# A graph network's edge products: split bf16 matmuls replaced by float32 matmuls over 64 rows

## The chip, the cores and the metric

One core of one Trainium2 chip. The metric is the device time of one execution in microseconds; the median of three runs of the kernel before is 1686.68 (1679.48 to 1689.82).

## The reference

Three layers of a graph network on 3125 nodes of 128 features, with 53125 directed edges sorted by destination, each with 64 attributes. Everything is float32. For layer k:

```
e   = edge_vector @ edge_W[k] + edge_b[k]      # 53125x64 @ 64x128
msg = relu(x[src] + e)
agg = segment_sum(msg, dst)
z   = (1 + eps[k]) * x + agg
h   = relu(batch_norm(z @ W1[k] + b1[k]))
x   = relu(layer_norm(h @ W2[k] + b2[k]))
```

The end result is the layer norm of the input plus the last x. The change touches how `edge_vector @ edge_W[k]` is computed for all three layers.

## The kernel before

The edges are cut into tiles of 128, four tiles a quad, four quads a block. Blocks alternate between two kinds. Those of kind s have their source rows fetched by one-hot matmuls and for that are re-sorted by source; those of kind p have them gathered by GpSimd's indirect DMAs. Two blocks, one of each kind, are a body; there are 13 bodies, 52 quads of each kind. In what follows "quad n" (0 to 51) means one quad of kind s with one of kind p.

The program has two stages. In the **first** the edge products for all three layers are made at once (64 attributes by 3 x 128 columns), one tile a PSUM bank with 384 columns, four banks for s and four for p:

- SP and ScalarE load the attributes, 64 partitions of 512 edges per kind and quad, three slots for each kind (`load_attr`, line 409).
- TensorE multiplies in bf16. A float32 number is written as a sum of three bf16 parts: the high half of the word is the first part in place, the remainder after it gives the second, the remainder after that the third. VectorE makes the remainders (`split_attr`, lines 958 to 969, two instructions per kind and quad, subtracting and writing the third part into the low halves), ScalarE copies the second and third parts to partitions 64 to 127 (`second_part`, lines 708 to 716, two per kind and quad), so that a matmul contracts 128 rows of two parts at once. The weights are split once (lines 975 to 982). TensorE then takes five accumulating bf16 matmuls per tile (`terms_of`, lines 1549 to 1557).
- Kind s is copied out of PSUM by ScalarE (line 734, all four banks at once), two columns of metadata are appended (line 738), and GpSimd scatters the rows by four indirect DMAs, one per tile, to a table in DRAM in source order (`srt`, line 668). Four buffers in `stage_s`; a quad's buffer is free again when the scatters of four quads earlier have landed.
- Kind p is evicted by VectorE with the bias added (`staged`, line 1124) and stored by SP to `ep` (line 445), with two buffers.
- VectorE has much else to do in between, in an order written out by hand by the quad's number: ranks and positions of the edges for the scatter (lines 1021 to 1055; the first positions before quad 0, lines 1355 to 1358), one-hot matrices (`hots_of`, line 1142; `build_hots`, line 1205), and the three-part split of x (lines 1169 to 1181).
- Before it there is a start: VectorE counts edges by source slice, TensorE ranks them (line 1539), VectorE works out a flag that picks this path or a general one (line 1086), on which all engines wait.
- In bodies 9 to 12 GpSimd's queue also has the four gathers of body 0 (line 652), each between two groups of scatters.

In the **second** stage each layer goes over the 13 bodies: one-hot gathers on TensorE (line 1582), additions on VectorE (lines 1220, 1227), relu on ScalarE (line 748), one-hot scatters on TensorE (line 1599 in bf16 for s, line 1609 in float32 for p), and the small node matmuls (lines 1618, 1625, 1633). Layer 0's later bodies need metadata that is read back after all of the first stage's scatters have landed (`load_meta`, line 454). Every engine runs its own instructions in program order, and semaphores join them.

## Time and profile before

| | |
|---|---|
| median of three runs | 1686.68 us |
| the profiled execution: span, first to last instruction | 1314.0 us |
| its own time beside the span | not given; median less span is 372.7 us |
| TensorE busy | 1201.3 us, 91% |
| VectorE busy | 1049.1 us, 80% |
| GpSimd busy | 886.4 us, 67% |
| ScalarE busy | 686.1 us, 52% |
| mean granted TensorE clock | 0.961 |
| DMA | 310.09 MB, mean 236 GB/s |
| chain that ended last, by engine | PE 46%, POOL 24%, issue 15%, DVE 11%, DMA 4% |

PE is TensorE, DVE VectorE, ACT ScalarE, POOL GpSimd. Busy shares are averages over stages that have different limits, so the rows below are read by stage. The first stage's products run on TensorE from 28 to 385 us; the rest is the three layers. A line in the trace has its start, its duration, the engine and the source line, and in brackets the idle time of that engine before it and what ended it.

### The profile page before, as it was taken

What the parts mean: (1) busy time and instruction counts of PE and PEld (TensorE: products, weight loads), DVE (VectorE), ACT (ScalarE), POOL (GpSimd) and SP (SyncE); (2) the same over time, 40 slices, a digit from 0 to 9 for tenths busy, and PEclk for the clock granted to TensorE, in tenths of its full rate; (3) what the DMA queues carried; (4) which work ended last, traced back from release to release, by engine and by line L of the source; (5) the groups of instructions that cost most, each with busy time, mean ns of one, the idle gap of its engine ahead of it and who ended that gap; (6) DMA issues with size and microseconds to landing.
All of it is one profiled execution on the core that took longest, in us unless ns stands there. A gap on an engine that the chain in (4) does not pass through costs nothing.

```text
span 1314.0 us, 36511 instructions
## 1 busy us (share of the span) xinstructions
PE 1201.3 (91%) x13740; PEld 1016.8 (77%) x13740; DVE 1049.1 (80%) x2020; ACT 686.1 (52%) x1303; POOL 886.4 (67%) x842
## 2 busy tenths in 40 slices
PE   3999999999996899999996899999996899999995
PEld 1555555555566899999986889999985898999994
DVE  8889988899877899998977566767666658788887
ACT  2665666666644466656552344444442434545543
POOL 0555666678777777777725777777762777777770
PEclk8999999999997899999997899999997999999997
DMA  8687888888988888888884777777766677788771
GB/s 181 236 275 259 282 293 284 294 292 266 320 268 266 263 246 251 247 250 245 242 265 139 209 217 228 228 224 228 231 199 181 176 226 211 238 242 250 240 215 35
DMA packets 253577, 310.09 MB, mean 236 GB/s; under 512 B 53837, under 2 KB 170623, under 8 KB 253415
## 3 DMA queue, kind: packets, MB, share of 16 engines
q1 hardware_dynamic: 205646, 212.37, 52.3%
q0 software_dynamic: 33280, 82.06, 19.9%
q10 hardware_dynamic: 14489, 13.40, 4.1%
q8 instruction: 115, 1.88, 0.6%
q14 instruction: 47, 0.39, 0.1%
HBM read 200.17 MB, written 107.55 MB: 234 GB/s over the span
## 4 chain that ended last, share of the span: by engine, by line
PE 46%; POOL 24%; issue 15%; DVE 11%; DMA 4%; ACT 1%; DVEq 0%; ACTq 0%; SPq 0%
POOL rows L652 20%; PE ps L1582 17%; PE ps L1609 6%; PE ps L1599 5%; POOL srt_dram L668 4%; PE ps L1553 3%; PE ps L1555 3%; PE ps L1554 3%; PE ps L1556 3%; PE ps L1557 3%; DMA rows<-table_dram,src_i 3%; DVE terms L966 1%; PE ps L1633 1%; DVE terms L1124 1%; DVE hot_stage L1142 1%
## 5 line engine op out<-in xcount | busy, mean ns | idle before, releaser
L652 POOL DMA_INDIRECT rows<-table_dram,src_i x416 | 431.9, 1038 | 182.0 <-issue 176.8
L668 POOL DMA_INDIRECT srt_dram<-region,pos_i x208 | 230.2, 1107 | 149.2 <-ACT region L738 62.9
L652 POOL DMA_INDIRECT rows<-x_dram,src_i x208 | 222.1, 1068 | 63.4 <-issue 63.4
L1582 PE MATMUL ps<-xs,early_words 125*128 125x128 bf16 x2720 | 253.4, 222 | 10.9 <-issue 10.9
L1582 PE MATMUL ps<-xs,region 125*128 125x128 bf16 x2584 | 242.5, 223 | 11.0 <-issue 10.8
L1582 PE MATMUL ps<-xr,early_words 125*128 125x128 bf16 x1360 | 243.6, 221 | 0.0
L1582 PE MATMUL ps<-xr,region 125*128 125x128 bf16 x1292 | 232.9, 222 | 0.0
L1582 PEld LDWEIGHTS ps<-xs,early_words 125*128 125x128 fp8e4 x2720 | 219.5, 99 | 11.3 <-issue 11.1
L1582 PEld LDWEIGHTS ps<-xs,region 125*128 125x128 fp8e4 x2584 | 209.6, 99 | 11.4 <-issue 11.1
L748 ACT ACTIVATE terms<-terms 128x512 f32<-128x512 f32 x156 | 97.4, 625 | 217.5 <-DVE terms L1220 217.4
L1609 PE MATMUL ps<-hot_p,terms 128*128 128x64 f32 x1248 | 170.5, 281 | 12.9 <-issue 12.3
L1609 PEld LDWEIGHTS ps<-hot_p,terms 128*128 128x128 f32 x1248 | 155.3, 196 | 21.0 <-issue 20.2
L1220 DVE TENSOR_TENSOR terms<-ps,terms 128x512 f32<-128x512 f32 x156 | 107.3, 688 | 79.5 <-PE ps L1582 74.3
L1227 DVE TENSOR_TENSOR terms<-rows,terms 128x512 f32<-128x512 f32 x156 | 107.0, 686 | 58.3 <-DMA rows<-table_dram,src_i 54.5
L1599 PE MATMUL ps<-hot_s,terms 128*128 128x144 bf16 x624 | 124.7, 228 | 25.2 <-DVE ps L1254 11.2
L1582 PEld LDWEIGHTS ps<-xr,early_words 125*128 125x128 fp8e4 x1360 | 133.1, 98 | 0.2
L1582 PEld LDWEIGHTS ps<-xr,region 125*128 125x128 fp8e4 x1292 | 127.1, 98 | 0.1
L1124 DVE TENSOR_TENSOR terms<-ps,eb_all 128x1536 f32<-128x1536 f32 x52 | 91.3, 1755 | 43.1 <-PE ps L1557 42.7
L1599 PE MATMUL ps<-hot_s,early_words 128*128 128x144 bf16 x624 | 124.6, 228 | 0.0
L1599 PE MATMUL ps<-hot_s,attr_x 128*128 128x144 bf16 x624 | 124.5, 228 | 0.0
L1236 DVE TENSOR_TENSOR attr_x<-terms 128x512 f32<-128x512 f32 x156 | 106.6, 683 | 14.9 <-ACT terms L748 13.0
L1238 DVE TENSOR_TENSOR early_words<-attr_x 128x512 f32<-128x512 f32 x156 | 107.9, 692 | 5.4
(194 smaller groups left out, 2565.8 us busy)
## 6 DMA issues: line engine op xcount, KB each, us to landing
ep_dram<-terms SPq DMA_DIRECT2D x52, 768.0 KB, 4.4
terms<-srt_dram SPq DMA_DIRECT2D x156, 256.0 KB
terms<-ep_dram SPq DMA_DIRECT2D x156, 256.0 KB
early_words<-hotrow_dram SPq DMA_DIRECT2D x156, 104.0 KB
region<-kept_dram SPq DMA_DIRECT2D x13, 576.0 KB
early_words<-kept_dram SPq DMA_DIRECT2D x13, 576.0 KB
region<-kept_dram SPq DMA_DIRECT2D x13, 560.0 KB
early_words<-kept_dram SPq DMA_DIRECT2D x13, 560.0 KB
```

The costliest lines, as they stand in the source:

```text
L652: pool.indirect_dma_start(rows[:, q, t * FEAT:(t + 1) * FEAT], None, source, bass.IndirectOffsetOnAxis(ap=src_i[:, c:c + 1], axis=0),).the ...
L668: pool.indirect_dma_start(srt, bass.IndirectOffsetOnAxis(ap=pos_i[:, c:c + 1], axis=0), stage_s[:, q, t, :], None).then_inc(scattered[q], 16)
L748: nc.scalar.activation(terms[:, q, :], terms[:, q, :], ACT.Relu).then_inc(s_relu, 1)
L1124: nc.vector.tensor_tensor(stage_p[:, n % 2, :].rearrange("p (l t d) -> p t l d", l=LAYERS, t=QUAD), ps[:, BLOCK_QUADS * BANK_COLS:8 * BANK ...
L1220: nc.vector.tensor_tensor(terms[:, q, :], bank(q), terms[:, q, :], ALU.add).then_inc(s_added, 1)
L1227: nc.vector.tensor_tensor(mine, rows[:, q, :], mine, ALU.add).then_inc(p_added, 1)
L1236: nc.vector.tensor_tensor(left, whole, high(whole, n), ALU.subtract).then_inc(s_rest, 1)
L1238: nc.vector.tensor_tensor(last, left, high(left, n), ALU.subtract).then_inc(s_parts, 1)
L1553: nc.tensor.matmul(cols, firsts, high(wf[:, :], n), start=True, stop=False, skip_group_check=True)
L1582: ins = nc.tensor.matmul(bank(q)[:, c:c + FEAT], hot_g[v % 2][0:SLICE, h, at:at + P], x_part(part, FIRST[t] + k), start=k == 0 and part == ...
L1599: ins = nc.tensor.matmul(ps[:, bass.ds(col, SORT_WINDOW)], part[:, t * FEAT:(t + 1) * FEAT], hot_s[:, q % 2, t * SORT_WINDOW:(t + 1) * SOR ...
L1609: ins = nc.tensor.matmul(ps[:, bass.ds(col, WINDOW)], terms[:, BLOCK_QUADS + q, t * FEAT:(t + 1) * FEAT], hot_p[:, q % 2, t * WINDOW:(t + ...
```

## The change

The edge products are made in float32 directly. A slot of `attr_x` holds both kinds: 128 partitions are loaded by one DMA of 256 KB, those of s in partitions 0 to 63, those of p in 64 to 127. For each of four tiles TensorE issues one matmul for s from the upper half and one for p from the lower, 64 contracted rows each, with the weights `wf`, which are in both halves. All splitting goes: of the weights, of the attributes on VectorE, and the copies on ScalarE. Evictions are made in halves: after two tiles of each kind the semaphores are raised, and ScalarE and VectorE take two banks each while TensorE fills the other two. The metadata copy comes ahead of the eviction, and GpSimd waits per two scatters for the half that it needs. All attribute loads are on SP's queue.

```diff
-        def load_attr(eng, n, kind):
-            b, q, slot = 2 * (n // BLOCK_QUADS) + kind, n % BLOCK_QUADS, n % ATTR_SLOTS
-            eng.dma_start(attr_t[kind][slot][0:EDGE_FEAT, :],
-                          attr[b * EDGE_FEAT:(b + 1) * EDGE_FEAT, q * QUAD * P:(q + 1) * QUAD * P]
-                          ).then_inc(attr_loaded[kind][slot], 16)
+        def half_of(n, half):
+            return 2 * n + half + 1
+        def load_attr(eng, n):
+            j, q, slot = n // BLOCK_QUADS, n % BLOCK_QUADS, n % ATTR_SLOTS
+            eng.dma_start(attr_x[:, slot, :], attr[j * P:(j + 1) * P, q * QUAD * P:(q + 1) * QUAD * P]
+                          ).then_inc(attr_loaded[slot], 16)
...
# SP, staged
-                sp.wait_ge(ep_filled, n + 1)
+                sp.wait_ge(es_filled, half_of(n, 1))
+                sp.wait_ge(ep_filled, half_of(n, 1))
                 if n + ATTR_SLOTS < LAYER_QUADS:
-                    load_attr(sp, n + ATTR_SLOTS, 1)
-                sp.wait_ge(ep_taken, n + 2)
+                    load_attr(sp, n + ATTR_SLOTS)
+                sp.wait_ge(ep_taken, half_of(n + 1, 1))
...
# GpSimd
-                        pool.wait_ge(es_staged, j * BLOCK_QUADS + q + 1)
                         for t in range(QUAD):
+                            if t % 2 == 0:
+                                pool.wait_ge(es_taken, half_of(j * BLOCK_QUADS + q + 1, t // 2))
...
# ScalarE, staged
-                if n + 1 < LAYER_QUADS:
-                    second_part(n + 1, 0)
                 if j >= 1:
                     act.wait_ge(scattered[q], j * 16 * QUAD)
-                act.wait_ge(es_filled, n + 1)
-                nc.scalar.activation(stage_s[:, q, :, 0:LAYERS * FEAT], ..., ACT.Copy).then_inc(es_taken, 1)
                 nc.scalar.activation(stage_s[:, q, :, LAYERS * FEAT:LAYERS * FEAT + 2], meta_u[:, c:c + QUAD, :],
-                                     ACT.Copy).then_inc(es_staged, 1)
-                if n + ATTR_SLOTS < LAYER_QUADS:
-                    load_attr(act, n + ATTR_SLOTS, 0)
-                if n + 1 < LAYER_QUADS:
-                    second_part(n + 1, 1)
+                                     ACT.Copy)
+                for half in range(2):
+                    tiles = slice(2 * half, 2 * half + 2)
+                    act.wait_ge(es_filled, half_of(n, half))
+                    nc.scalar.activation(stage_s[:, q, tiles, 0:LAYERS * FEAT], ..., ACT.Copy).then_inc(es_taken, 1)
...
# VectorE: the weight preparation, split_attr(0), split_attr(1) and split_attr(n + 2) removed; staged
-                shape = [P, QUAD, LAYERS, FEAT]
+                shape = [P, 2, LAYERS, FEAT]
                 dve.wait_ge(ep_stored[n % 2], 16 * (n // 2 + 1))
-                dve.wait_ge(ep_filled, n + 1)
+                for half in range(2):
+                    tiles = slice(2 * half, 2 * half + 2)
+                    dve.wait_ge(ep_filled, half_of(n, half))
+                    nc.vector.tensor_tensor(...)   # two banks with the bias, then_inc(ep_taken, 1)
...
# TensorE: terms_of removed; staged
+                n, width = j * BLOCK_QUADS + q, LAYERS * FEAT
+                slot = n % ATTR_SLOTS
+                pe.wait_ge(attr_loaded[slot], (n // ATTR_SLOTS + 1) * 16)
+                for half in range(2):
+                    pe.wait_ge(es_taken, half_of(n, half))
+                    pe.wait_ge(ep_taken, half_of(n, half))
+                    for t in range(2 * half, 2 * half + 2):
+                        cut = slice(t * P, (t + 1) * P)
+                        of_s = nc.tensor.matmul(bank(t, width), attr_x[0:EDGE_FEAT, slot, cut], wf[0:EDGE_FEAT, :],
+                                                start=True, stop=True, skip_group_check=True)
+                        of_p = nc.tensor.matmul(bank(BLOCK_QUADS + t, width), attr_x[EDGE_FEAT:P, slot, cut],
+                                                wf[EDGE_FEAT:P, :], start=True, stop=True, skip_group_check=True)
+                    of_s.then_inc(es_filled, 1)
+                    of_p.then_inc(ep_filled, 1)
```

## Rows read from the trace of the kernel before

**Rows 1.** Windows by stage: busy us per engine (instructions), granted clock, DMA share, GB/s.

```profile
38.00:385.00 347.00, 343.91 (x2039) 197.97 (x2038) 300.45 (x363) 226.53 (x303) 231.68 (x210) 1.00 0.85 284
385.00:405.00 20.00, 12.20 (x180) 11.96 (x179) 11.32 (x16) 4.47 (x9) 15.73 (x15) 0.83 0.91 275
440.00:680.00 240.00, 228.18 (x3212) 220.10 (x3212) 215.21 (x449) 146.63 (x304) 177.02 (x168) 0.99 0.83 249
```

**Rows 2.** TensorE's timeline: bf16 products, float32 matmuls; and line 1609's durations (ns).

```profile
57.41 0.33 PE L1553 MATMUL ps<-wf,hot_s 128*128 128x384 bf16 x1
57.58 0.33 PE L1554 MATMUL ps<-wr,hot_s 128*128 128x384 bf16 x1
...
521.50 1.10 PE L1609 MATMUL ps<-hot_p,terms 128*128 128x64 f32 x8 [0.69 <-issue]
...
525.01 0.65 PE L1625 MATMUL ps<-region,w_cur 128*128 128x121 f32 x4
...
L1609 PE MATMUL ps<-hot_p,terms x1248: 268/275/471, 403.6 to 1293.9; 128*128 128x64 f32 x179
```

**Rows 3.** The chain of waits after the last scatter: start, duration, what.

```profile
404.31 2.58 DMA srt_dram<-region,pos_i
...
438.93 0.91 PE ps L1599 x12
```

**Rows 4.** GpSimd's timeline in the first stage.

```profile
37.50 1.15 POOL L668 DMA_INDIRECT srt_dram<-region,pos_i  x1 [34.51 <-DVE pos_i L1055]
...
56.76 0.96 POOL L668 DMA_INDIRECT srt_dram<-region,pos_i  x1 [1.85 <-ACT region L738]
...
63.48 0.95 POOL L668 DMA_INDIRECT srt_dram<-region,pos_i  x1 [1.86 <-ACT region L738]
...
291.05 0.96 POOL L668 DMA_INDIRECT srt_dram<-region,pos_i  x1 [0.30 <-issue]
```

**Rows 5.** Waits from 38 to 385 us: total us, times, longest.

```profile
POOL srt_dram L668 <- ACT region L738: 62.9, 37, 3.1
```

**Rows 6.** VectorE's timeline in the start.

```profile
3.93 0.56 DVE L977 TENSOR_TENSOR wr<-wf 128x384 f32<-128x384 f32 x1 [0.65 <-DMA wf<-edge_w_dram]
...
6.49 0.14 DVE L988 CAST part_f<-part_i 128x1 f32<-128x1 int32 x1
...
17.77 0.68 DVE L966 TENSOR_TENSOR terms<-hot_p 64x512 f32<-64x512 f32 x1
...
20.43 0.46 DVE L1061 COPY region<-ps 128x312 f32<-128x312 f32 x1
...
28.27 0.68 DVE L966 TENSOR_TENSOR terms<-hot_s 64x512 f32<-64x512 f32 x1 [0.82 <-DVE flag L1086]
...
37.01 0.19 DVE L1055 CAST pos_i<-early_words 128x48 int32<-128x48 f32 x1
```

**Rows 7.** Groups by line, 28 to 386 us: count, busy us, mean ns, idle before.

```profile
L1124 DVE TENSOR_TENSOR terms<-ps,eb_all 128x1536 f32<-128x1536 f32 x52 | 91.3, 1755 | 43.1 <-PE ps L1557 42.7
L968 DVE TENSOR_TENSOR attr_x<-terms 64x512 bf16<-64x512 f32 x51 | 37.3, 731 | 1.7
L966 DVE TENSOR_TENSOR terms<-attr_x 64x512 f32<-64x512 f32 x51 | 34.1, 669 | 0.0
...
L738 ACT ACTIVATE region<-z_sum 128x8 f32<-128x8 f32 x52 | 10.5, 201 | 0.0
```

**Rows 8.** Windows again, as in rows 1, of stretches of ten microseconds.

```profile
100.00:110.00 10.00, 10.00 (x61) 5.78 (x60) 9.72 (x14) 7.12 (x9) 5.81 (x6) 1.00 0.79 281
340.00:350.00 10.00, 10.00 (x61) 5.82 (x60) 7.62 (x11) 7.50 (x10) 7.87 (x8) 1.00 1.03 378
398.00:409.00 11.00, 6.84 (x60) 6.85 (x61) 5.17 (x8) 4.45 (x8) 8.56 (x9) 0.53 0.77 249
```

**Rows 9.** The timeline of GpSimd and of VectorE at 342 us.

```profile
342.09 1.71 POOL L668 DMA_INDIRECT srt_dram<-region,pos_i  x1 [0.30 <-issue]
342.23 0.74 DVE L1142 TENSOR_TENSOR hot_stage<-iota_f,meta_s 128x576 fp8e4<-128x576 f32 x1
```

More of the change, by code:

```diff
@@ L141, in build @@
         wf = sb("wf", [P, LAYERS * FEAT])
-        wr = sb("wr", [P, LAYERS * FEAT])
-        wx = sb("wx", [P, LAYERS * FEAT])
-        wz = sb("wz", [P, LAYERS * FEAT], bf16)
         eb_all = sb("eb_all", [P, LAYERS, FEAT])
@@ L233, in build @@
         attr_x = sb("attr_x", [P, ATTR_SLOTS, QUAD * P])
-        attr_t = ((hot_p[:, :, :].rearrange("p h w -> p (h w)"),
-                   hot_s[:, :, :].rearrange("p h w -> p (h w)").bitcast(f32)[:, 0:QUAD * P],
-                   scratch_end[:, 0:QUAD * P]),
-                  tuple(attr_x[:, n, :] for n in range(ATTR_SLOTS)))
-        attr_r = terms[:, 6:8, :]
         rest_s = attr_x[:, 0:2, :]
@@ L297, in build @@
         weights_loaded = sem("weights_loaded")
-        attr_loaded = [[sem(f"attr_loaded{kind}{n}") for n in range(ATTR_SLOTS)] for kind in range(2)]
+        attr_loaded = [sem(f"attr_loaded{n}") for n in range(ATTR_SLOTS)]
         ident_zero = sem("ident_zero")
@@ L434, in _ @@
             for n in range(ATTR_SLOTS):
-                for kind in range(2):
-                    load_attr(sp, n, kind)
+                load_attr(sp, n)
             def staged(j, q):
                 n = j * BLOCK_QUADS + q
-                sp.wait_ge(ep_filled, n + 1)
+                sp.wait_ge(es_filled, half_of(n, 1))
+                sp.wait_ge(ep_filled, half_of(n, 1))
                 if n + ATTR_SLOTS < LAYER_QUADS:
-                    load_attr(sp, n + ATTR_SLOTS, 1)
-                sp.wait_ge(ep_taken, n + 2)
+                    load_attr(sp, n + ATTR_SLOTS)
+                sp.wait_ge(ep_taken, half_of(n + 1, 1))
                 sp.dma_start(ep[j * P:(j + 1) * P, :].rearrange("p (l c) -> p l c", l=LAYERS)
@@ L613, in _ @@
                 sp.dma_start(x_in, x[0:NODES_PAD, :].rearrange("(t p) d -> p t d", p=NT)).then_inc(xin_loaded, 16)
-                for kind in range(2):
-                    for slot in range(ATTR_SLOTS):
-                        sp.wait_ge(attr_loaded[kind][slot], 16)
-                sp.wait_ge(attr_mid, 4)
+                for slot in range(ATTR_SLOTS):
+                    sp.wait_ge(attr_loaded[slot], 16)
                 with sp.Fori(0, LAYERS) as l:
@@ L1547, in _ @@
             general = pe.value_load(flag[0:1, 0:1])
-            def terms_of(whole, t, cols):
-                cut, n = slice(t * P, (t + 1) * P), LAYERS * FEAT
-                firsts, thirds = high(whole, QUAD * P)[:, cut], low(whole, QUAD * P)[:, cut]
-                nc.tensor.matmul(cols, firsts, high(wf[:, :], n), start=True, stop=False, skip_group_check=True)
-                nc.tensor.matmul(cols, firsts, high(wr[:, :], n), start=False, stop=False, skip_group_check=True)
-                nc.tensor.matmul(cols, firsts, low(wf[:, :], n), start=False, stop=False, skip_group_check=True)
-                nc.tensor.matmul(cols, thirds, high(wx[:, :], n), start=False, stop=False, skip_group_check=True)
-                return nc.tensor.matmul(cols, thirds, wz[:, :], start=False, stop=True, skip_group_check=True)
@@ L1559, in staged @@
-            def staged(j, q):
-                n = j * BLOCK_QUADS + q
-                for kind, (taken, filled) in enumerate(((es_taken, es_filled), (ep_taken, ep_filled))):
-                    pe.wait_ge(attr_mid, n * 4 + (2 * kind + 2))
-                    pe.wait_ge(attr_low, n * 2 + (kind + 1))
-                    pe.wait_ge(taken, n + 1)
-                    for t in range(QUAD):
-                        ins = terms_of(attr_t[kind][n % ATTR_SLOTS], t, bank(kind * BLOCK_QUADS + t, LAYERS * FEAT))
-                    ins.then_inc(filled, 1)
+            def staged(j, q):
+                n, width = j * BLOCK_QUADS + q, LAYERS * FEAT
[12 more added lines that the diff above has]
+                    of_p.then_inc(ep_filled, 1)
```

68 lines of the change are left out of this document (14 added, 54 removed).

## The prediction

> **What bounds the kernel now.** First the windows: what each engine does in the stage that the change touches. From 38 to 385 us, the edge products, TensorE is busy 343.91 of 347 us at full clock, VectorE 300.45, GpSimd 231.68, and the DMA engines 85% [rows 1]. Then the spacing of TensorE's instructions: five bf16 matmuls of 384 columns per tile, each 0.17 us after the last (57.41, 57.58) [rows 2]. A quad is 8 tiles, 40 matmuls. GpSimd's starved groups, at 56.76 and 63.48, give that pace more exactly [rows 4]: 6.72 us a quad, 0.168 a matmul, 349 us for 52 quads, which is the stage. So TensorE sets the pace of the products.
>
> But the products are not what the kernel waits for. The chain of waits, read around the stage's end, leaves TensorE: the last scatter is issued at 404.31, lands, its metadata is read back, and from there VectorE's work leads to TensorE's scatter matmuls at 438.93 [rows 3]. Products end at 385; GpSimd ends its scatters 20 us later. GpSimd's queue says why. Early on the first scatter of each four waits 1.85 us for ScalarE's staged quad (56.76, 63.48); from 291.05 on no such wait is left, only the ordinary 0.30 between two scatters of 0.96 [rows 4]. GpSimd starts at 37.5, starves for 36 quads, and from there works without a pause. In the stage it waited 62.9 us in 37 waits for ScalarE's line 738 [rows 5]. An ordinary pause is 0.3, so the excess is 62.9 - 37 x 0.31 = 51.4 us. That, and an earlier start, is all that faster products can give: what follows is anchored to the last scatter.
>
> Layer 0 after 440 has TensorE busy 228.18 of 240 and is untouched [rows 1]; I take it, and the layers after it, as moving along unchanged.
>
> **TensorE.** Removed per quad: 40 bf16 matmuls. Added: 8 float32 matmuls of 384 columns. A float32 matmul is two records here: line 1609 has 8 for four tiles, 1.10 us for the 8 with 64 columns; line 1625 has 4 for two tiles of 121 columns, 0.65 us [rows 2]. So 16 records per quad. Nothing here streams 384 columns in float32. Lower bound: a record costs what one bf16 matmul does, 16 x 0.168 = 2.7 us per quad. Upper: the 121-column rows scaled, taking 0.275, a record's median duration on line 1609, for the last, (0.65 - 0.275)/3 = 0.125 per record, x 384/121 = 0.40, so 6.3 us. I take two bf16 passes a record, 16 x 0.336 = 5.4 us: 64 and 121 columns cost nearly the same per record (0.118 and 0.125), so part of the upper end is weight loading that 384 columns cover.
>
> The two kinds sit in different halves of the rows. No row shows whether their matmuls then run together. The Trainium skill ("TensorE: Matmul & The Clock Gate", Part 3, Packing small matmuls) says matmuls whose operands lie in distinct row groups run concurrently; by it a quad would be about 2.7 us, the lower bound. The sum is the same by both, since 5.4 is already under GpSimd's pace; it matters for the slower rival.
>
> **GpSimd.** It has 208 scatters and, before the last, 16 gathers, so 56 groups of four, none changed. From 37.5 to 405.3 (404.3 and 0.96) they take 367.8 us; without the excess, 367.8 - 51.4 = 316, mean 5.6 per group. TensorE at 5.4 keeps ahead of that: 52 x 5.4 = 281 from about 29 (below), done near 310.
>
> **The start.** VectorE loses the weight preparation (3.93 to 6.49, 2.6 us), the first split (17.77 to 20.43, 2.7) and the second, four instructions from 28.27, 2.7 more; positions are ready at 37.2 (37.01 + 0.19), just before the first scatter's 37.5 [rows 6]. The two splits are in VectorE's own line and count whole: 5.4. Of the 2.6 only part arrives, since VectorE next waits for TensorE's rank matmuls, whose pitch does not change; I take 1.1. Together 6.5, bounds 5.4 and 8.0. The first scatter starts near 31. The first product, which waits for the same flag as the second split (28.27), comes about 4 us earlier, at 24; with 5 us more for a first quad at the low clock, the count of 5.4 a quad starts at 29.
>
> **VectorE and ScalarE.** Splits in the stage: 4 instructions of 0.67 and 0.73 us per quad, 2.8 us [rows 7]. An eviction of 1.755 becomes two. The extra is one fixed cost, bounded by the tiny ScalarE copy of 8 elements, 0.20 us [rows 7], below by 0. VectorE goes from 300.45/51.6 = 5.8 us a quad to about 3.2; ScalarE loses four copies a quad. Both lie beside GpSimd's 5.6 and cost nothing while that stands; if GpSimd were done in under 3.2 us a quad they would show. The evictions read PSUM in halves, so TensorE refills one half while the other is drained; of a pace of 5.6, VectorE's evictions take 1.95 and leave 3.6 for its other work, which needs 3.2 - 1.95 = 1.3 on average, so only a large piece is felt, and four staged quads cover that.
>
> **Queues.** SP issues one 256 KB load in place of its 128 KB one, now behind a second wait (both kinds filled). Behind that wait is the store of the quad; both kinds finish together, so it adds nothing. ScalarE's queue loses its load and its issue time. Bytes are the same. The metadata copy moves ahead of the eviction; the scatter now waits for the eviction itself, 0.2 us sooner.
>
> **DMA gives some back.** Its work in 38 to 405 is 0.85 x 347 + 0.91 x 20 = 313 us of all engines [rows 1]. In 316 us that asks for a share of 0.99. Ten-microsecond stretches run from 0.79 to 1.03 [rows 8], so it can be reached, but hardly held for 300 us with two slots for the stores and four for the scatters. At 0.97 it takes 313/0.97 = 323 us, 7 more than GpSimd alone. I take 8. At 1.0, nothing; at 0.90, 348 us, 32 back.
>
> **Sum.** 51.4 + 6.5 - 8 = 50 us off the last scatter, from 405.3 to about 355. Span 1314.0 - 50 = 1264. The profile has no time beside the span; 1686.68 - 1314.0 = 372.7 us lie around it, taken as unchanged. The median becomes 1637.
>
> **GpSimd itself may get faster.** The scatter at 342.09 took 1.71 us rather than 0.96 while VectorE ran line 1142's operation with both inputs in SBUF [rows 9]; the splits are of the same kind. The Trainium skill ("SBUF — State Buffer", SBUF: two separate sides) says such an operation and a GpSimd one that reads SBUF block each other for a whole instruction; by it the removed splits would shorten groups. From the rows: groups at 4 x 1.26 = 5.04 would be 282 us, 34 less than 316. DMA's 313 forbids most of that, leaving about 8 at share 1.0, and some more if packets shorten. Hence a low end of 1620.
>
> **Rivals.**
> - *DMA is the bound and stays at 0.90.* For it: the stage's mean is 0.85 with TensorE pacing, and stores and scatters lose latency cover. Against: stretches above 0.95. Gain 51.4 + 6.5 - 32 = 26, 1661 us. Also the price if a float32 quad costs 6.3: the last scatter near 29 + 328 + 7 = 364, gain 41, 1646. Chance 0.15.
> - *Weight loads are not covered.* Each record then costs 0.11 + 0.336, a quad 7.1, the last product near 29 + 371 = 400 and the last scatter near 407: no change, 1687. Against: line 1609's 64 columns cost what 121 do, so streaming hides under loading and should the other way round. Chance 0.08.
> - *Slower: the clock falls in the stage.* Work with half of the rows idle may be taken as too little, and TensorE would run at 1.2 GHz, as from 398 to 409, where the granted clock was 0.53 after TensorE had waited [rows 8]. A record doubles to 0.67, a quad to 10.8, the stage to 560 us; the last scatter near 590 instead of 405 less the start, +180, 1865 us. It decides once a quad takes over 6.72 us, so only if the halves do not run together: together, 5.4 us at the low clock harms nothing. For it: nothing but the missing rows. Against: a serial TensorE is busy nearly without a pause, and in layer 0, with pauses, the clock was 0.99 [rows 1]. Chance 0.07.
>
> **How the numbers follow.** The forecast case, GpSimd and DMA sharing the bound, has 0.70 and its own range of 1620 to 1652. Slices of the first rival up to 1664 are added; 2 in 10 stay outside. A change under 1% (17 us) can't be told from none, as three runs lie 10 us apart. Faster by more: 0.70 + 0.15 = 0.85. Same 0.08. Slower 0.07.
>
> **What would show it.** Right: GpSimd's waits for ScalarE nearly gone from the second group on; first scatter at 31, last near 355; DMA share near 0.97 between; 33 to 35 us from the last scatter to TensorE's scatter matmuls in the steady state as before; layer 0 the same length. TensorE's record spacing tells 2.7 from 5.4. Wrong: GpSimd's first-of-four waits still over 1 us (products pace it); scatters of 2 to 4 us in long rows (DMA); granted clock near 0.5 in the stage; or a last scatter at 355 with the end not 50 earlier, which would mean that layer 0 was not anchored there.

## The result and the profile after

The changed kernel takes 1620.49 us in the median of four runs (1613.91 to 1631.21), the kernel before 1683.08 beside it (1675.57 to 1689.82): ratio 0.9643, 95% interval 0.9587 to 0.9699, a gain of 62.6 us where 50 were forecast. Two later comparisons gave 0.9626 (0.9603 to 0.9648) and 0.9609 (0.9534 to 0.9684).

The first lesson lies in the span. The profile of after has a span of 1620.8 us in a run of 1622.57: 1.8 us lie around it, not 372.7. The kernel before was profiled on a chip that runs it in about 1314 us (e1 below); its timed runs come from chips that take 1671 to 1698. Below these are **the quick chip** and **the slow chips** (four comparisons, on at least two chips that behave alike). Nothing but the times and the traces tells the two sorts apart; what makes them differ was not tested. So the trace of after must be set beside a trace of the kernel before from a slow chip as well, which is the run e9_before_third below.

Windows of after, in the columns of [rows 1]:

```profile
30.00:350.00 320.00, 191.84 (x818) 103.75 (x818) 176.96 (x215) 87.03 (x152) 231.86 (x219) 0.79 0.91 312
440.00:680.00 240.00, 193.44 (x2297) 174.75 (x2296) 155.37 (x324) 106.85 (x218) 124.93 (x124) 0.89 0.59 174
```

And of the kernel before on a slow chip:

```profile
30.00:350.00 320.00, 307.27 (x1798) 175.18 (x1796) 270.10 (x324) 199.73 (x268) 203.12 (x184) 0.99 0.80 266
440.00:680.00 240.00, 191.36 (x2220) 174.91 (x2219) 153.59 (x294) 99.16 (x194) 128.78 (x125) 0.85 0.59 177
```

Every engine but GpSimd has much less to do in the first stage, and the DMA engines have more; in layer 0 the two are alike, and both differ from [rows 1], where TensorE ran 3212 matmuls in the same 240 us.

TensorE's timeline of after, at the granted clock of 1.2 GHz (first four rows; 0.51 of full speed from 102 to 105 us) and at 2.4 GHz (last four; 1.00 from 107.5 to 111 us):

```profile
102.51 0.84 PE L1503 MATMUL ps<-wf,attr_x 64*128 64x384 f32 x1
102.58 0.84 PE L1505 MATMUL ps<-wf,attr_x 64*128 64x384 f32 x1
103.15 0.84 PE L1503 MATMUL ps<-wf,attr_x 64*128 64x384 f32 x1
103.22 0.84 PE L1505 MATMUL ps<-wf,attr_x 64*128 64x384 f32 x1
...
107.98 0.48 PE L1503 MATMUL ps<-wf,attr_x 64*128 64x384 f32 x1
108.01 0.48 PE L1505 MATMUL ps<-wf,attr_x 64*128 64x384 f32 x1
108.30 0.48 PE L1503 MATMUL ps<-wf,attr_x 64*128 64x384 f32 x1
108.34 0.48 PE L1505 MATMUL ps<-wf,attr_x 64*128 64x384 f32 x1
```

Line 1503 is kind s, line 1505 kind p. The record of p starts 0.03 to 0.07 us after that of s, so the two run together. Such a pair of records starts every 0.32 us; a quad has 8 pairs (8 matmuls of two records each), which is 2.6 us at 2.4 GHz, and 8 x 0.64 = 5.1 us at 1.2 GHz. In the kernel before a quad was 40 bf16 matmuls, 0.17 us apart [rows 2].

GpSimd's timeline of after, first and last scatter and the first long wait (compare [rows 4]):

```profile
29.66 1.16 POOL L655 DMA_INDIRECT srt_dram<-region,pos_i  x1 [26.67 <-DVE pos_i L1003]
...
71.61 0.96 POOL L655 DMA_INDIRECT srt_dram<-region,pos_i  x1 [3.95 <-ACT region L712]
...
357.69 1.41 POOL L655 DMA_INDIRECT srt_dram<-region,pos_i  x1 [0.30 <-issue]
```

GpSimd's scatters from 28 to 420 us, with their waits (count, busy, mean ns, idle before), in the kernel before on a slow chip:

```profile
L668 POOL DMA_INDIRECT srt_dram<-region,pos_i x208 | 228.8, 1100 | 166.6 <-ACT region L738 78.9 <-issue 53.1 <-DVE pos_i L1055 34.6
```

Its last scatter, from the timeline:

```profile
417.95 0.96 POOL L668 DMA_INDIRECT srt_dram<-region,pos_i  x1 [0.30 <-issue]
```

After:

```profile
L655 POOL DMA_INDIRECT srt_dram<-region,pos_i x208 | 221.0, 1062 | 113.7 <-issue 60.7 <-DVE pos_i L1003 26.7 <-ACT region L712 26.3
```

This is the whole account of GpSimd's queue, from one execution of each kernel. The last scatter goes from 417.95 to 357.69, 60.3 us earlier, and the span from 1684.2 to 1620.8, 63.4 shorter. Of the 60.3, the start gives 7.9 (34.6 to 26.7 of waiting for positions), the waits for ScalarE's staged quad 52.6 (78.9 to 26.3), and the scatters themselves 7.8 (228.8 to 221.0); 7.6 more ordinary pauses, where a wait for ScalarE stood before, take some back (53.1 to 60.7). That makes 60.7; the gathers between, 0.9 us longer, and rounding make the rest. The waits for ScalarE in the changed kernel vary: 26.3 us here, 31.0 and 31.3 beyond the first scatter's in its two other traces on slow chips.

Groups of after, which answer to lines 1124 and 734 of before ([rows 7] has the first):

```profile
L1071 DVE TENSOR_TENSOR terms<-ps,eb_all 128x768 f32<-128x768 f32 x104 | 97.1, 954 | 148.2 <-remote 78.2
L712 ACT ACTIVATE region<-ps 128x768 f32<-128x768 f32 x104 | 84.0, 812 | 230.6 <-PE ps L1503 105.0
```

Half an eviction takes VectorE 0.954 us; two of them 0.15 more than the whole one of 1.755. Most of its idle time ended with "remote", something that the trace of a slow chip doesn't name; on the quick chip (e2) the same line had no such waits, and waited 75.3 us for the landing of the stores to `ep`.

### The profile page after: what moved, and what is told of

It is laid out like the page before. It is cut to its first block, busy times and chain, and to the rows that moved or that the text cites. A ratio compares the mean times of both kernels' runs of the same rounds, so it can differ in the third digit from the quotient of the medians.

```text
span 1620.8 us, 33542 instructions
## 1 busy us (share of the span) xinstructions
PE 1189.3 (73%) x12492; PEld 1001.6 (62%) x12492; DVE 924.2 (57%) x1858; ACT 548.4 (34%) x1146; POOL 858.3 (53%) x842
## 4 chain that ended last, share of the span: by engine, by line
PE 62%; issue 19%; DVE 7%; another core or an unknown queue 6%; DMA 3%; ACT 1%; SPq 1%; ACTq 0%; DVEq 0%; POOL 0%
PE ps L1522 33%; PE ps L1549 10%; PE ps L1539 8%; PE ps L1503 6%; DMA ep_dram<-terms 2%; PE ps L1573 2%; DVE terms L1071 2%; PE ps L1558 1%; PE ps L1565 1%; PE ps L1571 1%; PE ps L1505 1%; DVE hot_stage L1089 1%; SPq L465 0%; DMA attr_x<-attr_dram 0%
## 5 line engine op out<-in xcount | busy, mean ns | idle before, releaser
L1522 PE MATMUL ps<-xs,early_words 125*128 125x128 bf16 x2720 | 295.2, 233 | 81.1 <-issue 67.5
L1522 PE MATMUL ps<-xs,region 125*128 125x128 bf16 x2584 | 286.1, 234 | 74.1 <-issue 73.1
L1522 PEld LDWEIGHTS ps<-xs,early_words 125*128 125x128 fp8e4 x2720 | 237.2, 105 | 89.7 <-issue 76.2
L1503 PE MATMUL ps<-wf,attr_x 64*128 64x384 f32 x416 | 194.2, 619 | 124.6 <-issue 67.0
L1522 PE MATMUL ps<-xr,early_words 125*128 125x128 bf16 x1360 | 270.5, 233 | 19.3 <-issue 19.0
L655 POOL DMA_INDIRECT srt_dram<-region,pos_i x208 | 221.0, 1062 | 113.7 <-issue 60.7
L1522 PE MATMUL ps<-xr,region 125*128 125x128 bf16 x1292 | 258.8, 233 | 27.3 <-issue 27.0
L1503 PEld LDWEIGHTS ps<-wf,attr_x 64*128 64x128 f32 x416 | 92.4, 236 | 213.1 <-issue 187.2
L1549 PE MATMUL ps<-hot_p,terms 128*128 128x64 f32 x1248 | 186.8, 290 | 33.3 <-issue 31.8
L1505 PE MATMUL ps<-wf,attr_x 64*128 64x384 f32 x416 | 195.6, 623 | 0.0
L1071 DVE TENSOR_TENSOR terms<-ps,eb_all 128x768 f32<-128x768 f32 x104 | 97.1, 954 | 148.2 <-remote 78.2
L712 ACT ACTIVATE region<-ps 128x768 f32<-128x768 f32 x104 | 84.0, 812 | 230.6 <-PE ps L1503 105.0
```

Of the source, the lines that this page charges most:

```text
L655: pool.indirect_dma_start(srt, bass.IndirectOffsetOnAxis(ap=pos_i[:, c:c + 1], axis=0), stage_s[:, q, t, :], None).then_inc(scattered[q], 16)
L712: nc.scalar.activation(stage_s[:, q, tiles, 0:LAYERS * FEAT], ps[:, 0:QUAD * BANK_COLS].rearrange("p (t c) -> p t c", t=QUAD) [:, tiles, 0 ...
L1071: nc.vector.tensor_tensor(stage_p[:, n % 2, :].rearrange("p (l t d) -> p t l d", l=LAYERS, t=QUAD)[:, tiles], ps[:, BLOCK_QUADS * BANK_COL ...
L1503: of_s = nc.tensor.matmul(bank(t, width), attr_x[0:EDGE_FEAT, slot, cut], wf[0:EDGE_FEAT, :], start=True, stop=True, skip_group_check=True)
L1505: of_p = nc.tensor.matmul(bank(BLOCK_QUADS + t, width), attr_x[EDGE_FEAT:P, slot, cut], wf[EDGE_FEAT:P, :], start=True, stop=True, skip_gr ...
L1522: ins = nc.tensor.matmul(bank(q)[:, c:c + FEAT], hot_g[v % 2][0:SLICE, h, at:at + P], x_part(part, FIRST[t] + k), start=k == 0 and part == ...
```

## The experiments

The last scatter is the measure throughout, beside the time. This table is drawn from the runs' timelines of GpSimd and their spans, one execution each; the runs are explained below it.

| run | last scatter starts | span | from it to the end |
|---|---|---|---|
| quick chip: before [rows 3] | 404.31 | 1314.0 | 909.7 |
| quick: e1_before_again | 404.35 | 1310.4 | 906.1 |
| quick: e2_kinds_in_turn | 336.97 | 1243.6 | 906.6 |
| quick: e3_splits_kept | 373.45 | 1281.8 | 908.4 |
| quick: e4_whole_evictions | 363.86 | 1274.5 | 910.6 |
| slow: e9_before_third | 417.95 | 1684.2 | 1266.3 |
| slow: after | 357.69 | 1620.8 | 1263.1 |
| slow: e5_after_again | 360.27 | 1627.5 | 1267.2 |
| slow: e6_three_stores | 355.95 | 1610.3 | 1254.4 |
| slow: e7_fewer_loads | 355.49 | 1610.7 | 1255.2 |
| slow: e8_matmuls_twice | 376.07 | 1648.3 | 1272.2 |
| slow: e10_after_third | 359.46 | 1618.3 | 1258.8 |
| slow: e11_three_of_five | 404.91 | 1660.7 | 1255.8 |
| slow: e12_in_turn_three_stores | 357.12 | 1619.5 | 1262.4 |

On either chip the rest of the program has one length, within 5 us on the quick chip and within 18 on the slow ones, whatever the first stage does. So the last scatter marks the end of the first stage well.

That the layers wait for it is shown on the quick chip alone, where the chain of waits that ended last leads through it, in the kernel before [rows 3] and in e2, and even there not in e4. On the slow chips the chain takes another way: VectorE's last eviction of kind p, its store, the loads from `ep`, and from there TensorE's first scatter matmuls. In the kernel before (e9):

```profile
421.38 1.77 DVE terms L1124
...
429.79 3.84 DMA terms<-ep_dram
...
435.92 1.64 PE ps L1599 x12
```

And in after:

```profile
356.04 0.97 DVE terms L1071
...
364.30 3.72 DMA terms<-ep_dram
...
370.31 0.93 PE ps L1539 x12
```

In e9 the last eviction begins 3.4 us after the last scatter. From the first scatter matmul to the end it is 1248.3 us in e9 and 1250.5 in after: the layers keep their length by this mark too, and it came 65.6 us earlier. In e5, e8 and e12 the chain also passes the store and the loads; in e6, e7, e10 and e11 it stays on TensorE, which goes from the products into the gathers. On the slow chips the last scatter moves along with the end without being what the end waits for.

**e1_before_again.** The kernel before, unchanged.

> The kernel before, unchanged, profiled once more. The profile of the changed kernel has a span of 1620.8 us in an execution of 1622.6, with bodies of the layers of 31 us; the profile of before that I argued from has a span of 1314.0, with bodies of 22, against runs of 1683. Theory: that profile shows an execution unlike the timed ones. Here the span is within 3 us of the time (about 1683), a body of the layers takes about 31 us, and the first stage is as I read it: last scatter near 405, 6.72 us a quad. Rival: the span is again near 1314 with 370 us around it, and the change itself lengthened the layers' bodies while something outside the span got shorter.

It ran in 1312.15 us beside seven runs of itself with a median of 1314.46, span 1310.4. Neither expectation fits: the span is near 1314, as in the rival, but nothing lies around it. So the span of 1314.0 was no part of a run of 1686: it was a whole run on a quicker chip. No sum over one trace could have shown it, but the 372.7 us without any record should have raised the question.

**e2_kinds_in_turn.** The changed kernel with the order of the products changed, per half.

```
                     for t in range(2 * half, 2 * half + 2):
                         ...
                         of_s = nc.tensor.matmul(...)
+                    for t in range(2 * half, 2 * half + 2):
+                        cut = slice(t * P, (t + 1) * P)
                         of_p = nc.tensor.matmul(...)
```

> The changed kernel with the two tiles of kind s of each half ahead of the two of kind p, so that neighbours mostly lie in the same half of the rows. In the changed kernel a pair runs together: two records per 0.323 us, 2.6 us a quad. Here I expect 7 slots of 0.323 per half in place of 4, some 4.5 us a quad. Theory (GpSimd and DMA set the last scatter, at 5.9 us a group): last scatter moves by less than 5 us, time within 8 us of 1620. Rival (running the halves together is what brought the gain): a quad's cost adds to waits in series, 1 to 2 us a quad, 50 to 100 us, 1670 or more.

1246.27 us beside 1314.46, ratio 0.9482 (0.9441 to 0.9524). TensorE's timeline of this run (line 1503 is s, 1507 is p):

```profile
100.92 0.56 PE L1503 MATMUL ps<-wf,attr_x 64*128 64x384 f32 x1
100.93 0.59 PE L1507 MATMUL ps<-wf,attr_x 64*128 64x384 f32 x1
101.31 0.48 PE L1503 MATMUL ps<-wf,attr_x 64*128 64x384 f32 x1
101.36 0.48 PE L1507 MATMUL ps<-wf,attr_x 64*128 64x384 f32 x1
```

Program order has two matmuls of s, four records, ahead of the first of p. Yet the first record of p starts 0.01 us after the first of s. The edit didn't take the running together away: a quad still takes 2.6 us at 2.4 GHz, not the 4.5 expected. So the run says nothing on what the running together is worth. What it does give is the changed kernel's work, in all but that order, on the quick chip: a gain of 68.2 us there. The changed kernel itself was never run on it; that the order makes little difference is seen on slow chips, where e12 and e6 differ in it alone (ratios 0.9590 and 0.9578). Its window:

```profile
30.00:350.00 320.00, 209.83 (x1110) 139.68 (x1110) 196.71 (x244) 96.50 (x168) 249.59 (x232) 0.82 0.98 333
```

The scatters in the view used above, of the kernel before on the quick chip and then of this run:

```profile
L668 POOL DMA_INDIRECT srt_dram<-region,pos_i x208 | 230.2, 1107 | 149.2 <-ACT region L738 62.9 <-issue 51.8 <-DVE pos_i L1055 34.5
L655 POOL DMA_INDIRECT srt_dram<-region,pos_i x208 | 222.6, 1070 | 89.7 <-issue 58.8 <-DVE pos_i L1003 26.6 <-ACT region L712 4.3
```

All of the wait for ScalarE is gone (62.9 in [rows 5], 4.3 here, which is 14 ordinary pauses), the DMA share is 0.98, and the scatters' busy time falls from 230.2 to 222.6. The account of the slow chips works here too: 58.6 from the waits for ScalarE, 7.9 from the start, 7.6 from the scatters, less 7.0 for more ordinary pauses, is 67.1 us of the 67.3 by which the last scatter came earlier.

**e3_splits_kept.** The changed kernel with VectorE's four splitting operations per quad left in, on tiles that nothing reads.

```
+                for kind in range(2):
+                    step(nc.vector.tensor_tensor(idle_b[:, :], idle_a[:, :], high(idle_a[:, :], QUAD * P), ALU.subtract))
+                    step(nc.vector.tensor_tensor(low(idle_a[:, :], QUAD * P), idle_b[:, :], high(idle_b[:, :], QUAD * P),
+                                                 ALU.subtract))
...
+                    if n + 2 < LAYER_QUADS:
+                        split_nothing()
```

> The changed kernel with VectorE's four splitting instructions per quad put back on idle buffers of its own (their result is used by nobody), 2.8 us a quad. Theory: VectorE goes from 3.4 to some 6.3 us a quad with its synchronisation and becomes the bound just above GpSimd's 5.9, and scatters are issued more slowly beside them: last scatter 10 to 30 us later, 1630 to 1650. Rival (only TensorE's products paced the stage): no change, 1620. Second rival (the splits were the whole cost): near 1683 less the start's 6, 1675.

1284.25 us, ratio 0.9779 (0.9733 to 0.9825); 38.0 us of e2's 68.2 are lost, more than the 10 to 30 expected (e2 and this run also differ in the order of the products). Its window:

```profile
30.00:350.00 320.00, 198.86 (x792) 109.97 (x794) 306.44 (x406) 84.54 (x148) 238.51 (x207) 0.78 0.90 300
```

Two of its waits in the window (total us, times, longest; the second holds the 26.8 for the first scatter):

```profile
PE ps L1515 <- DVE terms L1073: 119.2, 47, 4.9
...
POOL srt_dram L657 <- ACT region L714: 54.1, 29, 26.8
```

And its scatters:

```profile
L657 POOL DMA_INDIRECT srt_dram<-region,pos_i x208 | 240.1, 1154 | 108.6 <-issue 54.5 <-ACT region L714 54.1
```

The loss has two parts of like size. VectorE is busy 306.44 of 320 us and TensorE waits for its evictions, so GpSimd waits for ScalarE 27.3 us (54.1 less the 26.8 for the first scatter) against 4.3 in e2, less 4.3 us of ordinary pauses. And the scatters themselves take 1.154 us each against 1.070, 17.5 us over the 208. That is 36.2 of the 36.5 us by which the last scatter came later than in e2.

**e4_whole_evictions.** The changed kernel with all four banks of a kind handed over and evicted at once. The size of an eviction is that of the kernel before, but not the rhythm: there TensorE filled the four banks of one kind while those of the other were drained; here it fills both kinds together and then waits for both.

```
-            return 2 * n + half + 1
+            return n + 1
...
# ScalarE, and the like in VectorE and TensorE
-                for half in range(2):
-                    tiles = slice(2 * half, 2 * half + 2)
+                for half in range(1):
+                    tiles = slice(0, QUAD)
```

> The changed kernel with one eviction and one semaphore per quad and kind, as before. TensorE must then wait for the whole quad to be drained: 2.6 + 1.76 + some 0.3 = 4.7 us in series, plus whatever VectorE does between, 1.3 on average. Theory: 6.0 us a quad, about GpSimd's pace of 5.9, so 0 to 15 us later, 1620 to 1635. Rival (evictions in halves carry the change): back to over 6.7 us a quad, 1660 or more.

1277.26 us, ratio 0.9730 (0.9682 to 0.9779); 31.0 us of the 68.2 are lost, twice the most that the theory gave (0 to 15), and less than its rival. Its window:

```profile
30.00:350.00 320.00, 215.01 (x812) 118.78 (x814) 171.68 (x163) 77.73 (x101) 220.31 (x214) 0.77 0.93 308
```

TensorE's timeline, the first record of two quads in a row:

```profile
100.66 0.56 PE L1503 MATMUL ps<-wf,attr_x 64*128 64x384 f32 x1 [2.02 <-DVE terms L1071]
...
107.22 0.56 PE L1503 MATMUL ps<-wf,attr_x 64*128 64x384 f32 x1 [2.02 <-DVE terms L1071]
```

TensorE and VectorE take turns: 4.5 us of products, part of them at 1.2 GHz after the pause, then 2.02 of waiting for an eviction, a period of 6.56 here, where GpSimd's four scatters need 4 x 1.26 = 5.04.

**e5_after_again, e6_three_stores, e7_fewer_loads, e8_matmuls_twice** ran together on a slow chip, beside a median of 1690.16 for the kernel before.

> The changed kernel, unchanged, beside the kernel before. The kernel before took 1314 here lately and 1683 in the first comparison, with the same first stage and layer bodies of 22 and 31 us, so the two comparisons ran under different conditions. Theory: the first stage gains the same in both: first scatter near 30, last near 340 to 358, so 47 to 65 us of 1314, 1250 to 1267; the kernel with the kinds in turn (1246) is no slower than this one. Rival (running the halves together brings gain): this one is clearly faster than 1246, 1235 or less.

The changed kernel: 1627.60 us, 0.9626 (0.9603 to 0.9648). This comparison fell on a slow chip, so the times expected for 1314 don't apply; the last scatter, 360.27, is close to after's.

> The changed kernel with a third buffer for the stores of kind p, so that VectorE waits for the store of three quads earlier. In the profile of the changed kernel VectorE waited 35 us in 14 waits for such stores, up to 10.6 each, with the DMA engines at a share of 0.93. Theory (DMA's work is the bound, the waits are only how it shows): the last scatter moves by 0 to 8 us, and another wait (scattered rows, attributes) grows in its place. Rival (latency with two buffers is the bound, not throughput): 15 us or more are gained.

```
-                dve.wait_ge(ep_stored[n % 2], 16 * (n // 2 + 1))
+                dve.wait_ge(ep_stored[n % 3], 16 * (n // 3 + 1))
...
```

A third buffer for the stores to `ep`: 1615.68 us, 0.9578 (0.9513 to 0.9643). The interval overlaps with e5's. The last scatter is 4.3 us earlier than in e5 and 1.7 earlier than in after, and e12, with the same buffer, is level with after. The medians of e5 and e6 are 12 us apart, the rival said 15 or more. Not shown to help.

> The changed kernel without the attribute loads after the first three; later quads multiply the attributes of the first three again, so the output is not the reference's. It takes 49 loads of 256 KB, 12.8 of some 104 MB, off the DMA engines in the stage. Theory (DMA at its limit): the stage's traffic is 12% less, the last scatter comes 15 to 30 us earlier, down to GpSimd's own 5.1 to 5.3 us per group (56 groups, 290, last near 322). Rival (GpSimd alone, or waits between engines, bound it): under 5 us.

```
-                if n + ATTR_SLOTS < LAYER_QUADS:
-                    load_attr(sp, n + ATTR_SLOTS)
...
```

1620.66 us, 0.9601 (0.9577 to 0.9625), with products that are not the reference's, as expected of it. Its window:

```profile
30.00:350.00 320.00, 181.59 (x818) 96.20 (x818) 177.72 (x215) 86.60 (x152) 230.19 (x219) 0.79 0.79 272
```

The DMA share fell from 0.90 in e5 to 0.79, and the last scatter came only 4.8 us earlier, which is what the rival gave (under 5); the medians are 6.9 apart with intervals that overlap. On a slow chip the DMA's throughput is not what holds the scatters. On the quick chip, with its share of 0.98, this was not tried.

> The changed kernel with every product matmul issued twice into the same place, 32 records a quad, 5.2 us a quad at full clock with the halves together. Theory (TensorE has slack): last scatter within 8 us of the changed kernel's, since 5.2 is under the pace of 5.5 to 5.9 and the clock should fall less. Rival (TensorE's work is in series with the evictions): 1.3 to 2.6 us a quad, 65 us or more later.

```
+                        nc.tensor.matmul(bank(t, width), attr_x[0:EDGE_FEAT, slot, cut], ...)
+                        nc.tensor.matmul(bank(BLOCK_QUADS + t, width), attr_x[EDGE_FEAT:P, slot, cut], ...)
```

1636.27 us, 0.9671 (0.9642 to 0.9700). Each product made twice, 5.2 us a quad, which is what the products would take at 2.4 GHz if the two kinds ran one after the other. Its window:

```profile
30.00:350.00 320.00, 271.98 (x1558) 172.94 (x1556) 171.00 (x206) 82.30 (x147) 220.66 (x207) 0.95 0.89 296
```

Its scatters:

```profile
L655 POOL DMA_INDIRECT srt_dram<-region,pos_i x208 | 224.2, 1078 | 129.7 <-issue 58.6 <-ACT region L712 44.4 <-DVE pos_i L1003 26.8
```

The last scatter is 15.8 us later than in e5 in the executions profiled, of which this one was the longest of its four; the medians are 8.7 us apart and their intervals just touch. So the cost may be some 9 us, but it isn't clear of the noise; theory (within 8) and measurement can't be told apart, and the rival's 65 us did not come. The waits for ScalarE are 44.4 us against 26.3 to 31.3 in the changed kernel's traces. The granted clock was 0.95, with TensorE busy 272 of 320 us.

**e9_before_third, e10_after_third, e11_three_of_five** ran together, on a slow chip.

> The kernel before once more, to have it profiled on the chip of this call. So far it took 1314 us on one chip and 1690 on another, where only the changed kernel was profiled. Theory: the first stage is the same on both chips (last scatter near 405), and the difference lies in the layers, where TensorE pauses about 0.7 us between matmuls that wait for nothing. If this is the slower chip: bodies of 31 us, last scatter 405. Rival: the first stage is itself slower there, last scatter at 415 or later, which would explain why the gain measured there (63 us) is more than the 48 between 405 and 357.

One run of 1686.09 us, span 1684.2. The last scatter is at 417.95, 13.6 later than on the quick chip, as the rival had it, with the products ending at 412 rather than 385; the remaining 357 of the 370 us lie in the layers. There the page shows what is longer. Line 1582's groups, busy us, mean ns, idle before; on the quick chip:

```profile
L1582 PE MATMUL ps<-xs,early_words 125*128 125x128 bf16 x2720 | 253.4, 222 | 10.9 <-issue 10.9
L1582 PE MATMUL ps<-xs,region 125*128 125x128 bf16 x2584 | 242.5, 223 | 11.0 <-issue 10.8
```

On the slow one:

```profile
L1582 PE MATMUL ps<-xs,region 125*128 125x128 bf16 x2584 | 292.3, 237 | 75.5 <-issue 75.1
L1582 PE MATMUL ps<-xs,early_words 125*128 125x128 bf16 x2720 | 292.4, 232 | 60.5 <-issue 59.5
```

TensorE pauses between matmuls that wait for nothing that the profile shows; these two groups have 113 us more of such idle time and 89 us more of busy time, 202 of the 357. After has the same pauses:

```profile
641.08 0.22 PE L1522 MATMUL ps<-xr,region 125*128 125x128 bf16 x1 [1.06 <-issue]
641.14 0.22 PE L1522 MATMUL ps<-xs,region 125*128 125x128 bf16 x1
642.53 0.26 PE L1522 MATMUL ps<-xs,region 125*128 125x128 bf16 x1 [1.18 <-issue]
642.60 0.31 PE L1522 MATMUL ps<-xr,region 125*128 125x128 bf16 x1
```

> The changed kernel beside it. Theory: on the faster chip the last scatter is DMA's, with a share near 0.98, at 337 to 345, and the time is 1245 to 1255, a gain of 60 to 70, equal to that of the kernel with the kinds in turn (1246); on the slower one, the same as twice before, 1620 to 1628. Rival (halves together matter): below 1235 on the faster chip.

1619.03 us beside 1687.44, ratio 0.9609 (0.9534 to 0.9684); last scatter 359.46. On the slow chips the change thus takes 58 to 60 us off e9's last scatter (after, e5, e10), against 67.3 (404.31 to 336.97, by e2) on the quick one.

> The kernel before with the second and third of the five bf16 matmuls of each tile left out (the products then lack those parts; all splitting stays): 24 matmuls a quad, 4.03 us. It has TensorE's shorter work and the old evictions, splits and copies. Theory: VectorE becomes the bound, 5.8 us a quad as measured before plus its waits in series, last scatter at 370 to 385, so 20 to 35 us off 405. Rival (TensorE's pace was the whole limit, so this brings what the change brought): 345 or earlier, 60 us off. Second rival (the splits and copies were in series with the products): nothing, 400 or later.

```
-                nc.tensor.matmul(cols, firsts, high(wr[:, :], n), start=False, stop=False, ...)
-                nc.tensor.matmul(cols, firsts, low(wf[:, :], n), start=False, stop=False, ...)
```

1664.29 us beside 1687.44, ratio 0.9897 (0.9819 to 0.9974). Its window:

```profile
30.00:350.00 320.00, 217.10 (x1133) 110.10 (x1132) 278.13 (x336) 210.66 (x284) 231.89 (x193) 0.93 0.85 284
```

Its scatters:

```profile
L668 POOL DMA_INDIRECT srt_dram<-region,pos_i x208 | 249.0, 1197 | 130.6 <-issue 61.6 <-ACT region L738 34.6 <-DVE pos_i L1055 34.5
```

The last scatter is at 404.91, 13.0 earlier than in e9, less than the 20 to 35 expected. TensorE's work in the window fell by 90 us, the waits for ScalarE from 78.9 to 34.6; but each scatter now takes 1.197 us instead of 1.100, 20 us over the 208. Faster products alone bring about a fifth of the change's gain at the last scatter, 13.0 of 60.3, and a third by the medians of this comparison, 23 of e10's 68 us. The two differ since the layers here didn't wait for the last scatter: the last eviction of kind p, at 392.68, came 28.7 us earlier than in e9.

**e12_in_turn_three_stores.** e6 with e2's order, so one edit from each.

> The changed kernel with both edits tried so far that might help: per half the two matmuls of kind s and then the two of kind p, and a third buffer for the stores to ep. It is one edit away from the third-buffer kernel and one from the kinds-in-turn kernel, so it can be read beside whichever ran on a like chip. Theory 1 (the halves' running together is not needed; GpSimd, the scatters and the stores set the stage's end): as the third-buffer kernel where the before kernel takes 1680 to 1690 us, ratio 0.955 to 0.963, last scatter 353 to 360, TensorE busy about 15 to 25 us more in the stage; or, where the before kernel takes 1314, ratio 0.943 to 0.950, last scatter 332 to 338. Rival (where TensorE is interrupted by pauses, the products in turn are too slow for GpSimd): ratio 0.965 to 0.98, last scatter 365 to 385, and GpSimd's waits for ScalarE's eviction above 45 us. Rival 2 (the third buffer harms by more stores in flight beside the scatters): last scatter 5 to 15 us later than the kinds-in-turn kernel's 337 on a chip of 1314, ratio above 0.953.

1621.19 us beside 1690.27, ratio 0.9590 (0.9539 to 0.9642), last scatter 357.12: neither better nor worse than e5 or e6 by more than the intervals, as theory 1 had it. But TensorE was busy 186.81 us in the window, no more than after's 191.84, where that theory expected 15 to 25 more; that is e2's finding again, since the order in the program doesn't part the halves.

## Why the prediction came out right

**The number.** 1637 was forecast, and 1620.49 came out, at the very edge of the range, whose low end was 1620; another of the three comparisons gave 1619.03. The gain was a quarter larger than forecast. The kind of cause was right, several terms were not, and they cancelled in part.

**The anchor: right on the chip of the trace.** There the last scatter is what the layers wait for, before and in e2. On the slow chips it moves with the end, but the chain of waits goes by VectorE's last eviction (421.38 to 356.04). The layers kept their length either way. Two figures of the forecast can be set beside after: first scatter near 31 (measured 29.66), last near 355 (357.69). That the second fits is luck: it was reckoned from 404.31, and the kernel before has its last scatter at 417.95 on the chips that were timed.

**The 372.7 us around the span: wrong, and harmless.** Nothing lies there. The sum subtracted a gain found in one trace from a time made on another kind of chip. It worked because 357 of the 370 us sit in the layers, which the change doesn't touch. The other 13.6 are in the stage, where GpSimd waited 78.9 us for ScalarE, and [rows 5] has 62.9. TensorE was busy 10 us less there in the same window (307.27 on a slow chip, 317.04 of 320 on the quick one). There was more to win, but 26.3 us of it was left over.

**Where the forecast fell short.** By the account of the slow chips the waits gave 45.0 us net of pauses (52.6 - 7.6), less than the 51.4 of the sum; the start 1.4 more than its 6.5; the faster scatters 7.8, which the sum left out; and the 8 that the DMA engines were to take back, nothing. The last two are the 10 us between 50 and the 60.3 at the last scatter, and more; the further 2.3 up to 62.6 are within what the rest of the program varies by.

**The waits for ScalarE: right in kind.** The forecast took all of the excess, 51.4 us. On the quick chip just that went (e2: 58.6 less 7.0 of pauses). On a slow chip 52.6 went and 26.3 stayed, in 13 waits of up to 4 us; by the forecast's own signs such waits, over 1 us, would have meant that the products still set the pace.

**The start: 6.5 forecast, 7.9 measured**, within the 5.4 to 8.0 given. The first product began at 23.35, where 24 was forecast.

**A float32 quad: 5.4 taken, 2.6 measured at 2.4 GHz**, the lower bound. The rule of the Trainium skill ("TensorE: Matmul & The Clock Gate", Part 3, Packing small matmuls), by which matmuls in distinct row groups run at the same time, is what the trace shows, with starts 0.03 us apart. The step's conclusion, that the sum is the same by either value, is doubtful by e8: at 5.2 a quad the median was 8.7 us longer, and the last scatter 15.8 us later in one execution each. Comparing 5.4 with GpSimd's mean of 5.6 left out that TensorE doesn't work without a pause: in after it waited 54.9 us for VectorE's evictions, and the mean granted clock was 0.79.

**The splits and the halves: what they carry was not priced.** The prediction put both at nothing because they lie beside GpSimd's work, and gave the halves only their fixed cost. That cost is right (0.15 us a quad; 0 to 0.20 was given). But the sum rests on them, and each carries much of the gain: with whole evictions 31.0 us of the 68.2 are gone (e4), with the splits 38.0 (e3), and without both, products made shorter brought 13.0 of 60.3 at the last scatter (e11). What came next in line was VectorE, in e3, and the taking of turns, in e4. The parts do not add up to the whole. The copies that ScalarE lost (its busy time fell from 199.73 to 87.03 us in the window) were never put back alone, so what they carry is open.

**GpSimd gets faster: right.** The 208 scatters took 7.8 us less on a slow chip, 7.6 on the quick one, about the 8 that was put at the low end; in e11, where the same splits fell into a shorter time, they took 20 us more. The test is e3, which put the splits back: 1.154 us a scatter against 1.070, on one chip. The Trainium skill ("SBUF — State Buffer", SBUF: two separate sides) says that a VectorE operation with two SBUF inputs and a GpSimd operation reading SBUF exclude each other; by it the removed splits would shorten scatters, and the traces agree, with these figures and with 1.197, 1.100 and 1.062 us in e11, e9 and after.

**DMA gives 8 back: wrong on both chips, in different ways.** The quick chip reached 0.98 over 320 us, and GpSimd waited 4.3 us in all; nothing was given back. On the slow chip the share was 0.91, close to the rival's 0.90, but it isn't the bound: with a share of 0.79 the last scatter came 4.8 us earlier (e7). What stayed there instead were 26.3 us of waits for ScalarE. What holds ScalarE and VectorE is only partly named: VectorE waited 35.4 us for stores and 78.2 for something "remote", ScalarE 7.6 for landed scatters and 89.2 for something "remote", and TensorE paused 67.0 us on line 1503 for nothing that is shown.

**The rivals.** DMA at 0.90: its share came, its time (1661) didn't. Weight loads not covered: 2.6 us a quad excludes it. The clock: it did fall, to a mean of 0.79 in the stage ([rows 1] had 1.00), with whole quads at 1.2 GHz. As the rival's own condition had it, this does little harm where the halves run together: 5.1 us a quad.

## What to carry to other kernels

Before a span is subtracted from a time, ask whether both come from the same kind of chip; a gap between them that no record fills is a warning. Look also at which engine the chain of waits passes through in a trace of the kind of chip that is timed: the mark that moves with the end need not be what the end waits for. An engine that feeds the critical one through small buffers is not free at the mean pace: compare its work plus the hand-over and the eviction with the consumer's period, and ask of each part of a change what would bind without it. When small products are the work, operands in opposite halves of the rows let two matmuls run in the time of one, here whatever the order of issue; what it is worth has to be tested. Here the products made twice, in the time that the two kinds would take one after the other, cost some 9 us in the median, not clear of the noise (e8).

## What was not expected of the hardware

- The same program took 1314 us on one chip and 1687 on others. On the others TensorE pauses for about 1 us between matmuls that wait for nothing shown; before line 1582's two largest groups such idle time rose from 21.7 to 134.6 us. What causes them was not tested and stays open.
- Matmuls in different row halves start out of program order, as the trace has them: with two of s issued ahead of two of p, p's first record started 0.01 us after s's first (e2). The time agrees: the 4 pairs of a half still take 1.3 us at 2.4 GHz.
- A float32 matmul of 384 columns with 64 rows is two records, each 0.32 us after the last at 2.4 GHz and 0.64 at 1.2 GHz, while the other half of the rows does the same.
- Scatters issued by GpSimd took 1.154 us each with VectorE's splits beside them, and 1.070 without (e3, e2).
